# Who issues two kinds of stores: ScalarE behind its own copies, or SyncE, in a transformer block with routed experts

## What is computed

```python
x = x + attn(layernorm(x))     # 16 heads of 16, causal; softmax weights times a gate for each key
x = x + ffn(layernorm(x))      # 8 experts of 128, two for each row, and two shared blocks of 128
# attn: softmax(Q K^T / 4) * gate[key] @ V @ Wo + bo;  gate = tanh(g_w2 . gelu(drift * g_w1 + g_b1) + g_b2)
# ffn:  scores = sigmoid(x @ gate_w.T), 8 experts in 4 groups; the best 2 groups, then the best 2 experts,
#       weights normalised to 2.5; y = sum of w2 @ (silu(w1 x) * (w3 x)) * weight, plus the shared blocks
```

## Time and profile before

| | us |
|---|---|
| median of 3 runs | 1803.69 (1797.37 to 1806.76) |
| the profiled execution | 1808.59 |
| its span, first to last instruction | 1806.6 |

### The profile page before, as it was taken

One profiled execution on the slowest core, in us unless ns is written; L12 is line 12 of the kernel. 1 busy time (PEld: TensorE's weight loads), 2 busy tenths in 40 slices (PEclk: granted clock), 3 DMA queues, 4 the chain that ended last, 5 costly groups with the idle time before them and its releaser, 6 DMA issues.

```text
span 1806.6 us, 34673 instructions
## 1 busy us (share of the span) xinstructions
PE 1653.0 (91%) x12785; PEld 982.5 (54%) x12785; DVE 1292.4 (72%) x2528; ACT 1081.9 (60%) x1808; POOL 811.8 (45%) x1390
## 2 busy tenths in 40 slices
PE   7798989989988999899998989999999889999888
PEld 3344446435544566455654555555564557666677
DVE  5776767967795777777785757877688666963655
ACT  3466756665655655675656755586556765568432
POOL 5234533463345221632237863363207773157760
PEclk9699999999998999999998999999999999999999
DMA  5556655554445532644545665453535675336440
GB/s 151 158 156 194 176 169 152 182 153 124 125 127 147 158 104 87 174 113 120 159 118 151 185 194 152 127 162 108 147 93 172 198 197 159 97 129 199 135 122 13
DMA packets 192708, 261.25 MB, mean 145 GB/s; under 512 B 19616, under 2 KB 127264, under 8 KB 192544
## 3 DMA queue, kind: packets, MB, share of 16 engines
q1 hardware_dynamic: 181792, 229.67, 44.0%
q0 software_dynamic: 10752, 29.37, 5.6%
HBM read 130.98 MB, written 127.40 MB: 143 GB/s over the span
## 4 chain that ended last, share of the span: by engine, by line
PE 54%; DVE 14%; DMA 8%; ACT 8%; POOL 8%; issue 5%; SPq 3%; another core or an unknown queue 0%; POOLq 0%; ACTq 0%; DVEq 0%
PE ps_all L1961 10%; PE ps_all L2071 10%; DVE mx L1549 7%; PE ps_all L1941 6%; PE ps_all L1908 6%; PE ps_all L2102 5%; PE ps_all L1892 4%; ACT probs L1358 4%; PE ps_all L1878 3%; PE ps_all L1970 3%; POOL xs_s L1207 2%; PE ps_all L2081 2%; PE ps_all L2034 1%; DMA rr<-r_s 1%; DMA out<-rr 1%
## 5 line engine op out<-in xcount | busy, mean ns | idle before, releaser
L1549 DVE TENSOR_REDUCE mx<-ps_all 128x2 f32<-128x1024 f32 (+2 forms) x640 | 619.0, 1006 | 132.5 <-PE ps_all L1908 74.4
L1358 ACT ACTIVATE probs<-ps_all 128x1024 f32<-128x1024 f32 x576 | 571.8, 1028 | 218.0 <-PE ps_all L1941 209.9
L1175 POOL TENSOR_SCALAR_AFFINE_SELECT probs<-probs 128x256 f32<-128x256 f32 (+1 forms) x448 | 190.9, 443 | 495.5 <-ACT probs L1358 491.3
L1961 PE MATMUL ps_all<-probs,vaug 128*32 128x512 f32 (+3 forms) x3072 | 319.4, 516 | 21.9 <-POOL probs L1175 15.3
L1908 PE MATMUL ps_all<-k_st,q_st 63*128 63x512 f32 (+3 forms) x1536 | 269.3, 401 | 48.0 <-ACT probs L1358 16.3
L1941 PE MATMUL ps_all<-q_st,k_st 64*128 64x512 f32 (+3 forms) x1536 | 265.6, 401 | 29.3 <-ACT probs L1358 9.9
L1908 PEld LDWEIGHTS ps_all<-k_st,q_st 63*128 63x128 f32 x1536 | 135.1, 193 | 163.7 <-issue 52.2
L1941 PEld LDWEIGHTS ps_all<-q_st,k_st 64*128 64x128 f32 x1536 | 130.9, 191 | 158.9 <-issue 67.2
L2071 PE MATMUL ps_all<-w_hi,x2h 128*128 128x512 f32 (+1 forms) x480 | 168.2, 350 | 4.3 <-DVE x2l L1598 2.5
L1804 DVE SCALAR_TENSOR_TENSOR act_t<-act_t,ps_all 128x256 f32<-128x256 f32 x168 | 70.4, 419 | 123.4 <-ACT act_t L1421 110.9
L2071 PE MATMUL ps_all<-w_lo,x2h 128*128 128x512 f32 (+1 forms) x480 | 157.0, 327 | 0.0
(11 more groups left out here) (195 smaller groups left out, 2849.8 us busy)
## 6 DMA issues: line engine op xcount, KB each, us to landing
qk_s<-qh SPq DMA_DIRECT2D x116, 256.0 KB
q_st<-qk_s SPq DMA_DIRECT2D x128, 192.0 KB
k_st<-qk_s SPq DMA_DIRECT2D x128, 192.0 KB
xs<-xs_s SPq DMA_DIRECT2D x72, 256.0 KB
ys_s<-ysb SPq DMA_DIRECT2D x72, 256.0 KB
o_s<-o_sb SPq DMA_DIRECT2D x64, 256.0 KB
qk_s<-ql SPq DMA_DIRECT2D x57, 256.0 KB
xs_s<-ysb SPq DMA_DIRECT2D x20, 512.0 KB, 6.0
```

What stands on the lines that cost most here:

```text
L1175: last = nc.gpsimd.affine_select(out=block, in_=block, compare_op=ALU.is_ge, fill=0.0, base=0, pattern=[[0, heads], [1, P]], channel_multi ...
L1358: nc.scalar.activation(to, of, ACT.Exp, scale=DH ** -0.5).then_inc(freed[release[item][0]], 1)
L1549: last = nc.vector.tensor_reduce(to[:, :, p, qt % QPC], both[:, :, at:at + keys], X_AXIS, ALU.max)
L1961: last = mm(bank(first)[32 * h:32 * h + 32, q0 - c * CHUNK:], vaug[:, kt, g, h * VW:h * VW + 32], probs[:, s % 2, h, at:at + cols], start= ...
```

## The change

ScalarE issues both kinds of stores. `store_o` and `store_slots` move from SyncE's program to ScalarE's, with the same waits for the copy; the plan lists them there at a cost of 420 in place of 620. `o_sb` gets two halves, one for each chunk, so that a copy waits for the store of two chunks before. The second half takes 2 KB of each partition. To make room, `cmp_b` shrinks from eight squares to two, four small buffers move into unused squares of `cmp_a` and `cmp_b`, and `rank_op` no longer keeps two cubes at a time: it reduces each and adds the results, six steps in place of five, twice in each chain.

```diff
-RANK_OP = 13
+RANK_OP = 15
-DENSE_OPS = 19
+DENSE_OPS = 21
...
             add("ACT", ("OE", n, g, c), 466, due + 4000, [("PV", n, g, s)] + (
-                [("SO", (u - 1) // (GROUPS * CHUNKS), (u - 1) // CHUNKS % GROUPS, (u - 1) % CHUNKS)] if u else []),
+                [("SO", (u - 2) // (GROUPS * CHUNKS), (u - 2) // CHUNKS % GROUPS, c)] if u >= CHUNKS else []),
                 frees=(first, None))
-            add("SP", ("SO", n, g, c), ISSUE, due + 4000, [("OE", n, g, c)], lands=6000)
+            add("ACT", ("SO", n, g, c), 420, due + 4000, [("OE", n, g, c)], lands=6000)
...
-            ns = 620 if step in range(9, RANK_OP + 1) else 150
+            ns = 620 if step in range(10, RANK_OP + 1) else 150
...
-        add("SP", ("YS", n, u), ISSUE, due + 3500, [("YC", n, u)], lands=3000)
+        add("ACT", ("YS", n, u), 420, due + 3500, [("YC", n, u)], lands=3000)
...
-        o_sb = sb("o_sb", [P, CHUNK])
+        o_sb = sb("o_sb", [P, CHUNKS, CHUNK])
-        cmp_b = sb("cmp_b", [P, TILES, EXPERTS, EXPERTS])
+        cmp_b = sb("cmp_b", [P, 2, EXPERTS, EXPERTS])
-        slot_f = sb("slot_f", [P, 2, TILES])
+        slot_f, share = cmp_a[:, TILES - 2, 0:2, :], cmp_a[:, TILES - 1, 0:2, :]
...
-                if c:
-                    act.wait_ge(o_st[0], (gi + 1) * 16)
-                else:
-                    act.wait_ge(o_st[1], gi * 16)
+                if gi:
+                    act.wait_ge(o_st[c], gi * 16)
                 first = FIRST_STEP[c]
-                nc.scalar.copy(o_sb[:], bank(("PV", n, g, first))).then_inc(freed[release[item][0]], 1)
+                nc.scalar.copy(o_sb[:, c, :], bank(("PV", n, g, first))).then_inc(freed[release[item][0]], 1)
...
+            def store_o(item, n, g, c):
+                b, k = release["OE", n, g, c]
+                act.wait_ge(freed[b], k)
+                act.dma_start(o_s[bass.ds((n * GROUPS + g) * P, P), c * CHUNK:(c + 1) * CHUNK], o_sb[:, c, :]).then_inc(o_st[c], 16)
+
+            def store_slots(item, n, u):
+                b, k = release["YC", n, u]
+                act.wait_ge(freed[b], k)
+                if SET_OF[n] >= 2:
+                    for i in range(2):
+                        if first_wait(f"y_ld{i}", (CLOSES[SET_OF[n] - 2] + 1) * (TILES // 2 * 32)):
+                            act.wait_ge(y_ld[i], (CLOSES[SET_OF[n] - 2] + 1) * (TILES // 2 * 32))
+                act.dma_start(ys_s[SET_OF[n] % 2][bass.ds(u * Q, Q), :].rearrange("(t p) e -> p t e", p=P),
+                              ysb[:]).then_inc(ys_st, 16)
...
                 if r == 2:
-                    return nc.vector.tensor_tensor(b_, other, mine, ALU.is_gt)
+                    return nc.vector.tensor_reduce(to, a, X_AXIS, ALU.add)
                 if r == 3:
-                    return nc.vector.tensor_tensor(a, a, b_, ALU.add)
-                return nc.vector.tensor_reduce(to, a, X_AXIS, ALU.add)
+                    return nc.vector.tensor_tensor(a, other, mine, ALU.is_gt)
+                if r == 4:
+                    return nc.vector.tensor_reduce(others, a, X_AXIS, ALU.add)
+                return nc.vector.tensor_tensor(to, to, others, ALU.add)
```

More of the change, by code:

```diff
@@ L739, in build @@
             "count", "need", "room", "end", "row_old", "end_old", "jump"))
-        slot_f = sb("slot_f", [P, 2, TILES])
+        slot_f, share = cmp_a[:, TILES - 2, 0:2, :], cmp_a[:, TILES - 1, 0:2, :]
         slot_u = sb("slot_u", [P, 4, 2, TILES], mybir.dt.uint32)
-        owner, owner_old = sb("owner", [P, SLOT_TILES]), sb("owner_old", [P, SLOT_TILES])
+        owner = sb("owner", [P, SLOT_TILES])
+        owner_old = cmp_b[:, 0, :, :].rearrange("p a b -> p (a b)")[:, 0:SLOT_TILES]
         owner_i = sb("owner_i", [P, 2, SLOT_TILES], mybir.dt.int32)
-        share = sb("share", [P, 2, TILES])
         den = sb("den", [P, TILES])
@@ L973, in move_max @@
                                  ).then_inc(nm_in[g % 2][c], 16)
[L975 to L978, removed]
             def load_l(item, n, c):
@@ L1024, in load_slots @@
                     "(t p) e -> p t e", p=P)).then_inc(xs_ld[u % 2], 16)
[L1026 to L1034, removed]
             def load_rest(item, n, t):
@@ L1459, in _ @@
             all_work(act, "ACT", {"AN": norm_x, "CM": mix_scale, "GC": gate_norm, "CN": norm_rest, "AC": copy_xt, "QH": queries_keys, "GE": gelu1, "GI": gelu2, "GL": gate_tanh,
-                                  "MN": negate_max, "EX": exponent, "OE": copy_o, "CH": copy_hi, "XH": slots_hi,
+                                  "MN": negate_max, "EX": exponent, "OE": copy_o, "SO": store_o, "YS": store_slots, "CH": copy_hi, "XH": slots_hi,
                                   "CI": route_tanh, "RT": route_rows, "ET": expert_tanh, "HH": expert_high, "YC": copy_slots,
@@ L1601, in rank_op @@
             def rank_op(r, v, n_v, to, ts):
-                a, b_ = cmp_a[:, ts, 0:n_v, 0:n_v], cmp_b[:, ts, 0:n_v, 0:n_v]
+                a, others = cmp_a[:, ts, 0:n_v, 0:n_v], cmp_b[:, 0, 0:ts.stop - ts.start, 0:n_v]
                 cube = [P, ts.stop - ts.start, n_v, n_v]
@@ L1626, in choose_op @@
                     return nc.vector.tensor_tensor(grp[:, ts, :], pairs[:, :, :, 0], pairs[:, :, :, 1], ALU.add)
-                if r < 8:
+                if r < 9:
                     return rank_op(r - 3, grp[:, ts, :], EXPERTS // 2, rank_g[:, ts, :], ts)
-                if r == 8:
+                if r == 9:
                     return nc.vector.scalar_tensor_tensor(
@@ L1633, in choose_op @@
                         scalar=2.0, in1=sc[:, ts, :].rearrange("p t (g o) -> p (t g) o", o=2), op0=ALU.is_lt, op1=ALU.mult)
-                return rank_op(r - 9, sel[:, ts, :], EXPERTS, rank[:, ts, :], ts)
+                return rank_op(r - 10, sel[:, ts, :], EXPERTS, rank[:, ts, :], ts)
             def spread_op(r, ts):
@@ L1708, in slot_op @@
                     return nc.vector.tensor_reduce(slot_f[:, int(step[-1]), :], tmp, X_AXIS, ALU.add)
-                return nc.vector.tensor_copy(slot_u[:, n % 4, :, :], slot_f[:])
+                return nc.vector.tensor_copy(slot_u[:, n % 4, :, :], slot_f)
             def owner_op(n, step):
@@ L1722, in owner_op @@
                 if step in ("owner_old", "owner"):
-                    return nc.vector.tensor_reduce((owner_old if step == "owner_old" else owner)[:], ends, X_AXIS, ALU.add)
+                    return nc.vector.tensor_reduce(owner_old if step == "owner_old" else owner[:], ends, X_AXIS, ALU.add)
                 if step == "within":
-                    return nc.vector.scalar_tensor_tensor(out=owner_old[:], in0=owner_old[:], scalar=float(EXPERTS),
-                                                          in1=owner_old[:], op0=ALU.is_lt, op1=ALU.mult)
+                    return nc.vector.scalar_tensor_tensor(out=owner_old, in0=owner_old, scalar=float(EXPERTS),
+                                                          in1=owner_old, op0=ALU.is_lt, op1=ALU.mult)
                 if step == "both":
-                    return nc.vector.tensor_tensor(owner[:], owner[:], owner_old[:], ALU.add)
+                    return nc.vector.tensor_tensor(owner[:], owner[:], owner_old, ALU.add)
                 return nc.vector.tensor_scalar(owner_i[:, SET_OF[n] % 2, :], owner[:], float(EXPERTS - 1), float(2 * F),
```

4 lines of the change are left out of this document (2 added, 2 removed).

## The result

The changed kernel takes 1831.95 us, the median of four runs (1825.68 to 1834.71), against 1802.53 for the kernel before: a ratio of 1.0167, 95% interval 1.0134 to 1.0201. It is slower by 1.7%, and outside the forecast range. The profiled execution took 1834.71 us, its span 1833.0.

What follows compares the result with a forecast made beforehand. It saw many short TensorE gaps, TensorE waiting more for ScalarE than for SyncE's loads. +9.7 - 4.0 + 1 = +6.7 us on the median 1803.7 gave 1810.4, say 1811 us (chance 0.42); range 1790 to 1828.

Steps and rivals of the forecast that it cites:

- The price of one issue: On ScalarE's queue: 0.404 us of issue plus 0.13 us around the copy's end, 0.53 us; 136 make 72.6 us.
- The rival of dear issues: On ScalarE: half of the 136 issues take 1.78 us, giving 1822 to 1844 us, likeliest 1825; chance 0.18.
- The share of 13.4%: On ScalarE: a microsecond of its work lies on the path 13.4% of the time, so 72.6 us cost +9.7 us.
- That all is hidden: Rival: ScalarE's gaps hold the issues and the gain is filled too, -4 to +3 us, 1800 to 1807; chance 0.17.
- SyncE's gain: Stores no longer queue behind SyncE's loads, mainly in the last attention stretch: -4.0 us, ends 0 and -10.
- The rival that made SyncE's freed queue decide: Shorter waits for SyncE's loads, GpSimd's 69.2 us halved, make the kernel faster: -12.1 us, about 1792 us; chance 0.23.
- Halves 0, ranks +1 us: Sums' buffer: the wait for the store before is already hidden, 0; longer rank chains on VectorE: +1, ends 0 and +2.
- The new order: All queues planned anew: could shift gaps either way, priced by no row, called the largest reason for the range's width.
- the 136 short issues: Sign that the forecast is right: 136 issues of about 0.4 us on ScalarE's queue.
- TensorE's waits for exponents: Sign that the forecast is right: TensorE's waits for ScalarE's exponents go up by 5 to 15 us in sum.
- the wait of the copy of expert rows: Sign that the forecast is right: ScalarE's copy of expert rows waits for its store below 5.4 us.
- not within 1: Sign that the forecast is right: the store in the last stretch leaves within 1 us of its copy's end.

Runs made afterwards that it cites:

- e6: The kernel before with its lists kept, all 136 stores issued by ScalarE right behind their copies, ranks and buffers as before: ratio 1.0200.
- e9: The kernel before in its old lists, ScalarE issuing all 136 stores at the places where SyncE's list had planned them, mostly one to three items later: ratio 1.0015.
- e12: The kernel before in its old lists, SyncE issuing the stores, with the new ranks and the two halves of the sums' buffer: ratio 1.0013.
- e5: The kernel before in its old lists, SyncE issuing the stores, one buffer of sums, only the new ranks and the buffers moved for them: ratio 1.0028.
- e2: The changed kernel with its own lists, except that SyncE issues the 136 stores at the times planned for ScalarE: ratio 1.0113.
- e15: The whole change in the lists of the kernel before, ScalarE issuing each store where SyncE's list had planned it: ratio 1.0035.
- e13: The changed kernel with four small GpSimd multiplications added behind each scatter of batch 6: ratio 1.0089.
- e14: The kernel before with scatters 3 to 16 of batch 6 gathered in one run behind the five masks that stood among them: ratio 1.0047.

## Why the prediction was wrong, point by point

**The price of one issue: right.** 0.404 + 0.13 = 0.53 us was forecast for one that stands right behind its copy; e6 shows 0.52 and 0.55. The rival of dear issues fell with the answer to the earlier trace rows: 0.427 us at most, while SyncE went on issuing its own transfers. Its time, 1822 to 1844 us, holds the measured 1831.95 by luck. The wait for a shared generator, by which the Trainium skill (Perfetto Trace Analysis, DMA Instruction — HWDGE) gave a reason for that rival, does not show in these durations.

**The share of 13.4%: wrong as a rule.** Right behind the copies 36 of 72 us reach the end, one instruction later 2.7 us (0.15%, its interval holds 0). An average over all of ScalarE's work did not price a microsecond at a fixed place: behind the copies in the timelines an exponent was ready, and in e6 TensorE waited 16 us longer for exponents. That all is hidden, another rival, holds at e9's places and not right behind the copies. In the lists of the changed kernel 36 stores stand right behind their copies and most others one to four places later; there the issues cost 1.0167 - 1.0113 = 0.5%, 10 us, by runs whose intervals overlap. That the forecast had +9.7 us there confirms no share.

**SyncE's gain: wrong.** -4.0 us was for stores that leave sooner. In the changed kernel they leave at a median 0.03 us behind the copy's end, where it was 0.31 for the sums and already 0.03 for the expert rows; the latest leaves 8.1 us behind in place of 14.9, in the last stretch 2.9. In e6, where all leave within 0.03 us, ScalarE's wait for them fell from 5.4 us to 1.7, and the time rose. No run shows a gain. The rival that made SyncE's freed queue decide fell with GpSimd's waits, 74.0 us for 69.2. The stores have a queue of their own now (q10, 5.9% of the same 16 engines' time), and in e9 that gained nothing. This agrees with the Trainium skill (DMA: Bandwidth & Descriptors, Issuing engines are not separate DMA queues), by which issuing from several engines saves no more than the sequencer's time.

**Halves 0, ranks +1 us: near enough.** e12 has both for +2.3 us (interval -2.2 to +6.9), e5 the ranks for +5.0 (+1.3 to +8.8), more than the end of +2. The distance between copies of sums that hides the halves is 25 us (1591.7 us by 63), not 27.

**The new order: no term in the sum, and the step that failed.** The text called it the largest reason for the width and said that no row prices it; yet the sum took the order as kept, and the range ended at 1828. It cost 18 us by e2 and e12, 24 by the changed kernel and e15, the largest part of the 30 us lost in all, by either. Spacing the one run of scatters gave back 1.0167 - 1.0089 = 0.8%, 14 us (6 to 22 by the intervals; 4 to 9 were expected). In the two profiled executions, e13's being the slowest of its ten, it is less: from the first of these scatters to the end the changed kernel takes 234.7 us and e13 226.4, so 8 us are won, and TensorE's working time in the stretch accounts for 6 of them. And at 1578 us of the kernel before, ahead of the scatters, the changed kernel was already 14 us behind. So the run of scatters is a part of the price that is shown; what the lists lost before it, from 1176 to 1205 us above all, stays open.

The account of the 1.67%, by differences of runs and each uncertain by 0.3 to 0.6: ranks and halves 0.1 (e12), the new order 1.0 (e2 less e12), ScalarE's issues in it 0.5 (the changed kernel less e2). Of what the prediction asked the profile to show, the 136 short issues came true; TensorE's waits for exponents rose by 4.2 us, less than 5 to 15; the wait of the copy of expert rows rose to 10.4 us where it should have fallen, and in the last stretch five stores left 1.25 to 2.9 us behind their copies, not within 1.

## What to carry to other kernels

What an instruction cost here, on an engine with 40% idle time, depended on what stood right behind it, not on that engine's share of the path: look at the instruction that follows, and let it go first if another engine waits for it. Where a planner lays out all queues anew, give the new order a price of its own, and run the old order with the one edit beside it. A long run of scatters from GpSimd was worth breaking up; the old order did it with masks, which had to be made anyway, while added work behind every scatter cost more than it gave.

## What was not expected of the hardware

- Scatters 1.26 us apart, 14 or 15 in a row, hold up the other engines: TensorE 15.25 of 23 us in the changed kernel, and gaps of 1.0 to 1.7 us between matmuls of one accumulation in e14. The kernel before has eight in a row at the end of its stretch (1588.6 to 1600.3 us), and TensorE works 10.28 of those 11.7 us at full clock. Spaced 1.81 us apart in e13, TensorE works 21.32 of 23 us.

```profile
1588.60:1600.30 11.70, 10.28 (x76) 6.16 (x76) 7.89 (x10) 6.38 (x11) 7.71 (x8) 1.00 0.36 128
```

- Behind the fourteenth scatter of batch 6 GpSimd stood for 2.11 us, before and after, and 1.60 us in e13 where they are spaced.
- An issue on ScalarE's queue runs beside ScalarE's work: in e9 one of 0.34 us begins with an exponent at 1043.27, and the instruction behind follows without a gap.
- ScalarE's issues took 0.326 to 0.427 us, SyncE's for the same stores 0.320 to 1.890.
